# Eight output projections moved in among the last exponentials of the attention, with the divisor chain, the first routing slots and the key loads reordered around them

## The chip, the cores and the metric

One core of a Trainium2 chip (trn2). The metric is the device time of one execution in microseconds; lower is better. All four compute engines and the DMA queues run from their own instruction streams and meet only at semaphores.

## The reference, cut to what matters

Two transformer layers on x of shape (1, 2048, 256), all in float32. The change touches the end of the first layer's attention and the start of the second layer.

```python
xn = layernorm(x)                                    # over D = 256
q, k, v = split(xn @ w_qkv.T)                        # 16 heads of 16 columns
probs = softmax(mask(q @ k.T / 4))                   # causal, S = 2048
x = x + (probs @ v).reshape(S, 256) @ w_o.T + moe0(xn)   # top 2 of 16 experts
xn = layernorm(x)
probs = softmax(xn @ w_router); top 4 of 16 experts  # choices, weights
x = x + qn * sum(kn * v) + moe1(xn, choices) * 4/5 + (silu(xn @ ws1) * (xn @ ws3)) @ ws2 / 5
```

## The kernel before, in words

The kernel has three stages, each a block of five instruction streams. A block ends when every engine has reached its end.

**Stage one** (`stage_first`) computes the first layer. Tokens lie in 16 tiles of 128 and in four chunks c of 512; heads lie in four groups g of four. For each pair (g, c) it computes row maxima ("max" units: bf16 matmuls on TensorE, one `tensor_reduce` on VectorE), turns them ("turn"), and sends them by DMA into rows of the query tile (`rows_out`). Then come the exponentials: one "exp" unit is a score matmul for two heads and 128 keys (TensorE, into one of two banks `ps_st`), and one ScalarE `activation` of up to 1024 columns; one "pv" unit multiplies two such results by the values. There are 320 exps, numbered 1 to 320; (3, 3), the last pair, has 289 to 320. The units of the first expert layer (x, h, y, then fetch and sum) are threaded in between.

`attention_plan` works out one order of all units; every engine walks this same list and takes its own part of it in this order, so an instruction waits for all that stands ahead of it on its own engine. `with_shares` inserts further steps at given exp counts. These steps turn a chunk's raw head sums into attention output: for share n = (k, c), k = 0 or 1 being half of the heads, SyncE moves the softmax divisors out (`divisors_out`) and the heads to their place (`heads_home`), **gather** loads the divisors into `m.divisor` ([128, 32]), **invert** takes the reciprocal on VectorE, **return** stores it, **spread** loads it over the partitions in eight DMAs, and **share** multiplies on VectorE. There are eight shares (0 to 3: k = 0, 4 to 7: k = 1); the first seven are in stage one, and share 7 is in stage two.

SyncE walks the same list. A unit "exp" means nothing to it: it doesn't wait at one, so its DMAs leave as fast as the waits between them allow. At the turn of (g, 2), g at least 1, it waits for the values of group g - 1 and issues the six DMAs of `load_keys` for group g + 1 (each 256 KB, one for each of TERMS = 6 products of bf16 parts). For g = 1 there follow the two loads of the output weights `m.wo` (tensors `count` and `before`), and gather 0.

**Stage two** (`stage_second`) projects the 16 tiles of attention output (`project(i)`: two fp32 matmuls of 256 columns, and a VectorE addition to `m.x`), takes the second layer norm of each tile (VectorE `bn_stats`, `bn_aggr`; a square root on ScalarE in `root_of(c)`; `scales(c)` on VectorE; `normalize` on ScalarE), turns it (`turn`), scores it against the router (`score`, which waits for both DMAs of `w_in`: the router and `w_attn`), picks the experts (`best_of(c)`), counts ranks on TensorE (`ranks(c)`), and works out a slot in memory for every choice (`slots_of(c)`). GpSimd then sends every token row to its slots: 64 indirect DMAs, 16 for each chunk, which wait for `slots_ready` of that chunk and for nothing else but each other. TensorE meanwhile adds up a Gram matrix (`add_gram`) and does 16 units of the shared expert. When the 64 DMAs have landed, SyncE loads the first four tiles of rows (`m.xs`), and the block ends.

In stage two VectorE has this order, written by hand: tiles 0 to 4, scales 0, tiles 5 to 7, invert 7, tile 8, scales 1, tile 9, best_of 0, tile 10, share 7, slots_of 0, tile 11, tile 12, and so on. TensorE: project 0 to 6, turn 0 and 1, project 7, turn 2 and 3, project 8 and 9, score 0 to 3, project 10, add_gram 0 and 1, turn 4 and 5, ranks 0, add_gram 2, turn 6 and 7, project 11, score 4 to 7, project 12, and so on.

**Stage three** (`stage_experts`) runs the experts tile by tile and is not touched.

Of the kernel before, what the change touches and what calls it, by code (L numbers as in the profile page):

```python
# [333 lines left out]
def load_keys(eng, m, g, tokens, done):  # L334

    for t in range(TERMS):
        src = m.qk_parts[K_PART[t], D + g * HG * HD:D + (g + 1) * HG * HD, tokens]
        eng.dma_start(m.ks[g % 2][t * HD:(t + 1) * HD, :, tokens], src.rearrange("(h d) t -> d h t", d=HD)).then_inc(done, 16)
# [36 lines left out]
def common(nc, m):  # L375
# [30 lines left out]
    m.o_now, m.divisor = flat[:, 0:CH], m.r["slotf"][:, TOP0:TOP1, :].rearrange("p k i -> p (k i)")  # L406
# [267 lines left out]

SHARE_STEPS = (("gather", 3), ("invert", 13), ("return", 14), ("spread", 17), ("share", 28))
SHARES_FROM, SHARES_SPACE = 290, 2


def with_shares(plan):


    exps = [u for u in plan if u[0] == "exp"]
    due, at, n = [], 0, 0
    for u in plan:
        if u[0] == "exp":
            at += 1
        elif u[0] == "pv":
            g, c, k, _ = exps[2 * u[1]][1:]
            if g % 2 and k == TC * (c + 1) - 1 and n + 1 < len(SHARES):
                assert SHARES[n] == (g // 2, c)  # L690
                due += [(max(at + later, SHARES_FROM + SHARES_SPACE * n) if name == "share" else at + later, name, n)
                        for name, later in SHARE_STEPS]
                n += 1
    due.sort(key=lambda step: step[0])
    out, at = [], 0
    for u in plan:
        out.append(u)
# [8 lines left out]
NOT_ROWS = ("exp", "pv", "sum", "fetch", *(name for name, _ in SHARE_STEPS))  # L706
# [59 lines left out]
def stage_first(nc, m, a):  # L766
# [6 lines left out]
    row_of = {u[0:2]: n for n, u in enumerate(rows) if u[0] in "xhy"}  # L773
    rank_at = rows.index(("rank",))
    assert plan[TURNED - 1] == ("turn", 0, 0) and all(u[0] == "max" for u in plan[:TURNED - 1])
    with ExitStack() as ctx:
# [73 lines left out]
        def ends_pair(m):  # L850

            return exps[2 * m][3] == TC * (exps[2 * m][2] + 1) - 1
# [4 lines left out]

        def used(n):

            return sum(u[0] != "h" for u in rows[:n + 1])  # L860
# [8 lines left out]
        def _(sp):  # L869
# [19 lines left out]
            n = 0  # L889
            for u in plan:  # L890
                if u[0] == "pv" and ends_pair(u[1]):
# [8 lines left out]
                elif u[0] == "gather":  # L900
                    if u[1] == 0:
                        sp.wait_ge(slots_ready, TOP0 + 1)
                        for k in range(KH):
                            sp.dma_start(m.wo[k], a["w_o_t"][k * P:(k + 1) * P, :]).then_inc(m.wo_in, 16)
                    gather_divisors(sp, m, u[1])
                elif u[0] == "return":
                    return_divisors(sp, m, u[1])
                elif u[0] == "spread":
                    spread_divisors(sp, m, u[1])
                elif u[0] == "turn":  # L910
                    g, c = u[1:3]
                    if n:
                        rows_out(sp, n, c)
                    n += 1
                    if g + 1 < NG and c == (1 if g == 0 else 2):

                        if g >= 1:
                            sp.wait_ge(pv_done, last_pv(g - 1, C - 1))
                        load_keys(sp, m, g + 1, slice(0, S), k_in[(g + 1) % 2])
                    if (g, c) == (1, 0):  # L920

                        clear(sp, m, m.xd1, E * CAP // P, E * CAP // P + 1, m.cleared[1])
# [231 lines left out]
        def _(dve):  # L1154
# [73 lines left out]
            for u in plan:  # L1228
# [11 lines left out]
                if u[0] in ("pv", "gather", "return", "spread"):  # L1240
                    continue
                if u[0] == "sum":
# [16 lines left out]
                if u[0] == "x":  # L1259
# [40 lines left out]
        def _(pe):  # L1300
# [91 lines left out]
            for u in plan:  # L1392
# [44 lines left out]
                elif u[0] == "turn":  # L1437
# [3 lines left out]
                    mm = pe.transpose(bank[0:HG * TC, 0:P], neg_max[:, :], m.ident[:, :])  # L1441
                elif u[0] == "x":
# [287 lines left out]
def stage_second(nc, m, a):  # L1730
# [3 lines left out]
    with ExitStack() as ctx:  # L1734
# [68 lines left out]
        def _(sp):  # L1803
            last = len(SHARES) - 1
            divisors_out(sp, m, NG - 1, C - 1)
            sp.dma_start(wr[:, :, :], a["w_router"].rearrange("(k p) e -> p k e", p=P)).then_inc(w_in, 16)
# [51 lines left out]
        def _(act):  # L1858
# [14 lines left out]
            heads_home(act, m, NG - 1, C - 1)  # L1873
# [23 lines left out]
        def _(dve):  # L1897
# [23 lines left out]
            def project(i):  # L1921

                dve.wait_ge(w_done, i + 1)
                dve.tensor_tensor(m.x[:, i, :], ps_w[i % 2], m.x[:, i, :], ALU.add).then_inc(added, 1)
# [45 lines left out]
            slots_of(0)  # L1970
            tile(11)
            tile(12)
# [117 lines left out]
        def _(pe):  # L2090
# [31 lines left out]
            def project(tiles):  # L2122

                for i in tiles:
                    pe.wait_ge(m.shared, C + i // TC + 1)
                    if i >= 2:
                        pe.wait_ge(added, i - 1)
# [14 lines left out]
            project(range(10, 11))  # L2142
# [149 lines left out]
```

## Time and profile before

| | us |
|---|---|
| median of 3 runs | 903.83 |
| lowest, highest | 898.98, 904.56 |
| the profiled execution, its own time | 906.89 |
| its span in the trace | 905.2 |

| engine | busy us | share of the span |
|---|---|---|
| PE (TensorE matmul) | 830.5 | 92% |
| DVE (VectorE) | 645.3 | 71% |
| ACT (ScalarE) | 468.8 | 52% |
| POOL (GpSimd) | 437.1 | 48% |

Times in the trace count from the span's start. Stage one ends at 602, stage two at 731. The busy share is an average over stages that have different limits; what a change is worth is read where the change is. PEclk is the clock that TensorE was granted, 1.00 being 2.4 GHz and 0.50 being 1.2 GHz.

### The profile page before, as it was taken

What the parts mean: (1) busy time and instruction counts of PE and PEld (TensorE: products, weight loads), DVE (VectorE), ACT (ScalarE), POOL (GpSimd) and SP (SyncE); (2) the same over time, 40 slices, a digit from 0 to 9 for tenths busy, and PEclk for the clock granted to TensorE, in tenths of its full rate; (3) what the DMA queues carried; (4) which work ended last, traced back from release to release, by engine and by line L of the source; (5) the groups of instructions that cost most, each with busy time, mean ns of one, the idle gap of its engine ahead of it and who ended that gap; (6) DMA issues with size and microseconds to landing.
All of it is one profiled execution on the core that took longest, in us unless ns stands there. A gap on an engine that the chain in (4) does not pass through costs nothing. (4 is left out here: it accounts for less than half of the span.)

```text
span 905.2 us, 16683 instructions
## 1 busy us (share of the span) xinstructions
PE 830.5 (92%) x4934; PEld 449.4 (50%) x4935; DVE 645.3 (71%) x1472; ACT 468.8 (52%) x883; POOL 437.1 (48%) x720
## 2 busy tenths in 40 slices
PE   5978699999988999999999998989999989999993
PEld 3533133334533444444444432138644769888982
DVE  5587988898867888888788888437547336555648
ACT  2643154556654666666565666754313046555547
POOL 3422045603652433653435446531578848878820
PEclk9997698999998999999999999989999989999997
DMA  9654772210272121272211222325852235555566
GB/s 328 212 129 137 207 142 89 89 46 25 81 128 71 49 61 56 80 127 71 70 38 38 55 60 76 93 65 188 302 166 88 88 117 164 157 154 159 158 255 246
DMA packets 70182, 110.05 MB, mean 122 GB/s; under 512 B 16662, under 2 KB 49942, under 8 KB 69590
## 3 DMA queue, kind: packets, MB, share of 16 engines
q1 hardware_dynamic: 49430, 54.04, 22.9%
q0 software_dynamic: 16000, 45.70, 14.7%
q10 hardware_dynamic: 4672, 9.34, 3.4%
q8 instruction: 38, 0.62, 0.3%
q14 instruction: 42, 0.34, 0.1%
HBM read 62.53 MB, written 46.22 MB: 120 GB/s over the span
## 5 line engine op out<-in xcount | busy, mean ns | idle before, releaser
L1275 DVE TENSOR_REDUCE part_max<-ps_row 128x1 f32<-128x512 f32 (+3 forms) x560 | 353.6, 670 | 71.1 <-PE ps_row L1429 38.7
L1139 ACT ACTIVATE probs<-ps_st 128x1024 f32<-128x1024 f32 (+3 forms) x320 | 278.2, 896 | 204.6 <-PE ps_st L1408 188.2
L1333 PE MATMUL ps_o<-probs,v_all 128*17 128x512 f32 (+3 forms) x1280 | 150.4, 542 | 6.9 <-POOL probs L1009 5.6
L1429 PE MATMUL ps_row<-ks,qs 96*128 96x512 bf16 (+3 forms) x320 | 110.2, 379 | 13.7 <-DVE part_max L1275 9.3
L1429 PE MATMUL ps_row<-xt_ks,qs 96*128 96x512 bf16 (+3 forms) x320 | 104.5, 354 | 6.9 <-DVE part_max L1275 6.5
L1682 POOL DMA_INDIRECT yd<-moe_ys,moe_home x79 | 82.6, 1046 | 25.5 <-POOL moe_home L1676 13.4
L1408 PE MATMUL ps_st<-qs,ks 99*128 99x512 bf16 (+3 forms) x320 | 88.7, 360 | 2.9 <-DMA qs<-max_parts 2.7
L1408 PE MATMUL ps_st<-qs,xt_ks 99*128 99x512 bf16 (+3 forms) x320 | 85.7, 356 | 3.9 <-ACT probs L1139 2.8
L1702 PE MATMUL moe_ps_h<-moe_xs_t,moe_w_now 128*128 128x128 f32 x632 | 86.0, 280 | 1.3 <-ACT moe_xs_t L1607 0.8
L1702 PEld LDWEIGHTS moe_ps_h<-moe_xs_t,moe_w_now 128*128 128x128 f32 x632 | 78.4, 195 | 3.2 <-DVE moe_w_now L1569 2.0
L1429 PEld LDWEIGHTS ps_row<-ks,qs 96*128 96x128 bf16 x320 | 31.9, 100 | 95.6 <-DVE part_max L1275 52.8
L1009 POOL TENSOR_SCALAR_AFFINE_SELECT probs<-probs 128x256 f32<-128x256 f32 x128 | 52.8, 419 | 47.3 <-ACT probs L1139 46.0
L1851 POOL DMA_INDIRECT xd<-xn,slot x64 | 65.8, 1029 | 19.0 <-issue 15.9
L1019 POOL TENSOR_SCALAR moe_h_tanh<-moe_h_tanh 128x128 f32<-128x128 f32 x47 | 25.0, 532 | 98.7 <-ACT moe_h_copy L1151 98.5
L1429 PEld LDWEIGHTS ps_row<-xt_ks,qs 96*128 96x128 bf16 x320 | 31.0, 97 | 80.7 <-DVE part_max L1275 46.6
L1642 DVE TENSOR_TENSOR moe_hid_t<-moe_ps_h,moe_act 128x128 f32<-128x128 f32 x79 | 23.0, 291 | 47.7 <-ACT moe_act L1614 37.2
L997 POOL DMA_INDIRECT xd<-o_t,slot x32 | 31.4, 982 | 46.2 <-ACT probs L1139 41.7
L1432 PE MATMUL ps_row<-mask,ident 128*128 128x128 bf16 x256 | 51.7, 227 | 0.0
L1711 PE MATMUL moe_ps_y<-we,moe_hid_t 128*128 x158 | 48.6, 389 | 3.1 <-DVE moe_hid_t L1642 1.6
L1408 PEld LDWEIGHTS ps_st<-qs,xt_ks 99*128 99x128 bf16 x320 | 27.3, 99 | 47.8 <-ACT probs L1139 27.0
L1029 POOL DMA_DIRECT2D yd<-moe_ys x47 | 28.5, 605 | 46.1 <-DVE moe_ys L1267 45.4
L1333 PEld LDWEIGHTS ps_o<-probs,v_all 128*17 128x17 f32 x1280 | 21.7, 95 | 53.6 <-issue 29.0
(288 smaller groups left out, 1307.3 us busy)
## 6 DMA issues: line engine op xcount, KB each, us to landing
moe_xs<-xd SPq DMA_DIRECT2D x79, 129.0 KB
qk_parts<-probs SPq DMA_DIRECT2D x16, 384.0 KB, 4.2
qs<-qk_parts SPq DMA_DIRECT2D x96, 64.0 KB, 2.5
moe_xs<-xd POOLq DMA_DIRECT2D x47, 128.0 KB, 2.4
yd<-moe_ys POOLq DMA_DIRECT2D x47, 128.0 KB, 2.1
xd<-zeros POOLq DMA_DIRECT2D x2, 2048.0 KB, 15.5
moe_w<-in_w ACTq DMA_DIRECT2D x2, 2048.0 KB
w<-in_we SPq DMA_DIRECT2D x8, 512.0 KB
```

Of the source, the lines that this page charges most:

```text
L997: pool.indirect_dma_start(out=m.xd0, out_offset=bass.IndirectOffsetOnAxis(m.r["slot"][:, choice, i:i + 1], 0), in_=m.xn[:, i, :], in_offse ...
L1009: pool.affine_select(out=corner, in_=corner, compare_op=ALU.is_ge, fill=keep, base=0, pattern=[[0, 2], [1, P]], channel_multiplier=-1).the ...
L1139: act.activation(probs[:, at % NPB, :, off:CH], ps_st[at % 2][:, :, off:CH], ACT.Exp, scale=HD ** -0.5).then_inc(exp_done, 1)
L1275: dve.tensor_reduce(part_max[reduced % 2][:, h:h + k, i, j:j + 1], bank[:, 0:k * w].rearrange("p (h w) -> p h w", h=k), AX_X, ALU.max).the ...
L1333: mm = pe.matmul(ps_o[32 * q:32 * q + HD + 1, off:CH], m.v_all[:, k, g * HG + q, :], probs[:, (at + q // 2) % NPB, q % 2, off:CH], start=F ...
L1408: mm = pe.matmul(ps_st[n % 2][:, h, off:CH], ks[g % 2][:, q, k * P:(k + 1) * P], qs[c][:, q, off:CH], start=True, stop=True)
L1429: mm = pe.matmul(cols, qs[c][0:KROWS, h, i * P:(i + 1) * P], ks[g % 2][0:KROWS, h, j * CH:j * CH + w], start=True, stop=(j < c))
L1432: mm = pe.matmul(cols[:, w - P:w], m.ident16[:, :], m.mask16[:, :], start=False, stop=True)
L1682: pool.indirect_dma_start(out=yd, out_offset=bass.IndirectOffsetOnAxis(home[:, k:k + 1].bitcast(U32), 0), in_=ys[:, k % U, :], in_offset=N ...
L1702: mm = pe.matmul(ps_h[b][:, part * P:(part + 1) * P], w_now[:, b, k, part * HID:(part + 1) * HID], xs_t[:, b, k, :], start=(k == 0), stop= ...
L1711: pe.matmul(ps_y[b][:, :], hid_t[:, b, :], w2[:, bass.ds(expert, 1), :], start=True, stop=True).then_inc(y_done, 1)
L1851: pool.indirect_dma_start(out=m.xd1, in_=xn[:, i, :], in_offset=None, out_offset=bass.IndirectOffsetOnAxis(r["slot"][:, k, i:i + 1], 0)).t ...
```

## The change

Eight of the sixteen projections become plan units of stage one: `("project", i)` for tiles 0 to 7, after exps 297, 299, ... 311, in the row banks `ps_row`. Each adds to `m.x` on VectorE. Two units "moments" (after 306 and 313) do the `bn_stats` and `bn_aggr` of tiles 0 to 3 and 4 to 7 there. Shares 4, 1, 5, 2, 3, 6 get exp counts of their own. `m.divisor` gets memory of its own. In stage two the last heads move from ScalarE's queue to SyncE's, ahead of the router load, gather 7 and `w_attn`; TensorE starts with projections 8 and 9; VectorE starts with scales 0, and does slots_of 0 ahead of share 7. The six key DMAs of groups 2 and 3 are given exp counts three apart, and SyncE issues each when it meets that count in its list. By the list, the first two of group 2 come ahead of the output weights and gather 0, the next three behind gather 0, and the last behind return 0.

```diff
-SHARES_FROM, SHARES_SPACE = 290, 2
+KEY_SPACE = 3
+SHARES_AT = {0: 290, 4: 291, 1: 293, 5: 294, 2: 306, 3: 308, 6: 312}
+PROJECT_AT = (297, 299, 301, 303, 305, 307, 309, 311)
+MOMENTS_AT = (306, 313)
+BEFORE_LAST = len(PROJECT_AT)
...
-                due += [(max(at + later, SHARES_FROM + SHARES_SPACE * n) if name == "share" else at + later, name, n)
+                due += [(max(at + later, SHARES_AT[n]) if name == "share" else at + later, name, n)
...
+    due += [(at, "project", i) for i, at in enumerate(PROJECT_AT)] + [(at, "moments", c) for c, at in enumerate(MOMENTS_AT)]
...
             for u in plan:
-                if u[0] == "pv" and ends_pair(u[1]):
+                if u[0] == "exp":
+                    at += 1
+                    while pieces and pieces[0][0] <= at:
+                        _, g, t = pieces.pop(0)
+                        load_keys(sp, m, g, slice(0, S), k_in[g % 2], [t])
+                elif u[0] == "pv" and ends_pair(u[1]):
...
-                    if g + 1 < NG and c == (1 if g == 0 else 2):
-
-                        if g >= 1:
-                            sp.wait_ge(pv_done, last_pv(g - 1, C - 1))
-                        load_keys(sp, m, g + 1, slice(0, S), k_in[(g + 1) % 2])
+                    if (g, c) == (0, 1):
+                        load_keys(sp, m, 1, slice(0, S), k_in[1])
+                    if g + 1 < NG and g >= 1 and c == 2:
+
+                        sp.wait_ge(pv_done, last_pv(g - 1, C - 1))
+                        pieces += [(at + KEY_SPACE * t, g + 1, t) for t in range(TERMS)]
...
+                if u[0] == "moments":
+                    cs = slice(u[1] * TC, (u[1] + 1) * TC)
+                    dve.wait_ge(row_used, used(row_of["project", u[1] * TC + TC - 1]))
+                    for i in range(cs.start, cs.stop):
+                        step(dve.bn_stats(m.stat["bn"][:, i, :], m.x[:, i, :]))
+                    step.sync()
+                    for i in range(cs.start, cs.stop):
+                        step(dve.bn_aggr(m.stat["mv"][:, i, :], m.stat["bn"][:, i, :]))
...
+                if u[0] == "project":
+                    i = u[1]
+                    dve.wait_ge(summed, (i + 1) * TOP0)
+                    dve.tensor_tensor(m.x[:, i, :], bank[:, 0:D], m.x[:, i, :], ALU.add).then_inc(row_used, 1)
...
+                elif u[0] == "project":
+                    i = u[1]
+                    bank_free(n)
+                    pe.wait_ge(m.wo_in, 16 * KH)
+                    pe.wait_ge(m.shared, shares_upto(i // TC))
+                    for k in range(KH):
+                        mm = pe.matmul(bank[:, 0:D], m.o_t[:, 2 * k, i * P:(i + 1) * P], m.wo[k],
+                                       start=(k == 0), stop=(k == KH - 1))
...
             divisors_out(sp, m, NG - 1, C - 1)
+            heads_home(sp, m, NG - 1, C - 1)
             sp.dma_start(wr[:, :, :], a["w_router"].rearrange("(k p) e -> p k e", p=P)).then_inc(w_in, 16)
...
-            heads_home(act, m, NG - 1, C - 1)
...
-            for i in range(0, 5):
-                tile(i)
             scales(0)
-            for i in range(5, 8):
-                tile(i)
-            invert_divisors(dve, m, last)
             tile(8)
             scales(1)
             tile(9)
+            tile(10)
+            invert_divisors(dve, m, last)
             best_of(0)
-            tile(10)
-            share_heads(dve, m, last)
             slots_of(0)
             tile(11)
+            share_heads(dve, m, last)
             tile(12)
...
-            pe.wait_ge(m.wo_in, 16 * KH)
-            project(range(0, 7))
+            project(range(8, 10))
             turn(range(0, 2))
-            project(range(7, 8))
+            project(range(10, 11))
             turn(range(2, 4))
-            project(range(8, 10))
             pe.wait_ge(w_in, 32)
             pe.wait_ge(ones_ready, 1)
             score(range(0, 4))
-            project(range(10, 11))
             add_gram(range(0, 2))
```

## Rows read from the trace of the kernel before

**Rows 1.** Busy us of each engine (instructions), clock, DMA share, GB/s, by stretch.

```profile
268.20:274.20 6.00, 0.01 (x1) 0.01 (x1) 0.96 (x3) 0.39 (x1) 1.25 (x4) 0.86 0.69 154
274.20:280.20 6.00, 6.00 (x28) 2.96 (x29) 4.25 (x8) 1.93 (x3) 1.15 (x2) 0.57 0.23 67
```

**Rows 2.** Timeline of SyncE's queue: start, us, DMA issues and their count.

```profile
255.54 3.59 SPq L338 DMA_DIRECT2D ks<-qk_parts  x6
...
260.13 0.46 SPq L734 DMA_DIRECT2D slotf<-den  x1
```

**Rows 3.** DMA issues of 254 to 275: count, KB each, median us to landing.

```profile
ks<-qk_parts SPq DMA_DIRECT2D x6, 256.0 KB, 8.6
```

**Rows 4.** Timeline of the engines at 273 to 277; idle time before, and releaser, in brackets.

```profile
273.24 0.35 DVE L755 RECIPROCAL slotf<-slotf 128x32 f32<-128x32 f32 x1 [6.08 <-DMA slotf<-den]
...
274.19 0.61 PE L1429 MATMUL ps_row<-xt_ks,qs 96*128 96x512 bf16 x1 [6.00 <-DVE part_max L1275]
...
276.54 1.02 ACT L1139 ACTIVATE probs<-ps_st 128x1024 f32<-128x1024 f32 x1 [7.93 <-PE ps_st L1408]
```

**Rows 5.** Timeline of the last pair's exponentials, TensorE and ScalarE.

```profile
578.04 1.04 PE L1408 MATMUL ps_st<-qs,xt_ks 99*128 99x512 bf16 x4
...
578.69 3.89 ACT L1139 ACTIVATE probs<-ps_st 128x1024 f32<-128x1024 f32 x4 [0.26 <-PE ps_st L1408]
579.01 1.05 PE L1333 MATMUL ps_o<-probs,v_all 128*17 128x512 f32 x8
...
580.00 1.29 PE L1408 MATMUL ps_st<-qs,xt_ks 99*128 99x512 bf16 x4
...
587.18 3.77 ACT L1139 ACTIVATE probs<-ps_st 128x1024 f32<-128x1024 f32 x4 [2.40 <-remote]
```

**Rows 6.** Stretches, columns as in rows 1: exps 297 to 312, and stage two's second part.

```profile
574.53:594.87 20.34, 17.97 (x97) 3.18 (x96) 6.88 (x14) 15.40 (x17) 12.06 (x13) 0.92 0.32 92
...
647.90:727.20 79.30, 79.28 (x229) 42.42 (x225) 39.70 (x73) 16.16 (x24) 60.25 (x78) 1.00 0.35 118
```

**Rows 7.** Timeline of TensorE's projections, at the lower clock and at the full one.

```profile
605.03 1.06 PE L2129 MATMUL ps_ab<-before,o_t 128*128 128x256 f32 x2
...
608.21 0.59 PE L2129 MATMUL ps_o<-count,o_t 128*128 128x256 f32 x2
...
608.64 0.59 PE L2129 MATMUL ps_o<-before,o_t 128*128 128x256 f32 x2
```

**Rows 8.** Timeline of the DMA issues at the start of stage two.

```profile
602.81 2.57 ACTq L724 DMA_DIRECT2D o_t<-masks  x4
...
606.80 0.34 SPq L734 DMA_DIRECT2D slotf<-den  x1
...
607.18 0.43 SPq L1808 DMA_DIRECT2D w_attn<-in_w_attn  x1
```

**Rows 9.** DMA issues of 590 to 740: count, KB each, median us to landing.

```profile
w_attn<-in_w_attn SPq DMA_DIRECT2D x1, 768.0 KB, 4.6
```

**Rows 10.** Timeline from the square root's table to GpSimd's first dispatch.

```profile
605.42 1.28 ACT L1861 ACT_TABLE_LOAD   x1 [2.94 <-issue]
...
616.34 1.85 PE L2106 MATMUL ps_l<-w_router,xt 128*128 128x16 f32 x16
...
622.27 0.69 DVE L763 TENSOR_TENSOR o_t<-o_t 128x512 f32<-128x512 f32 x1 [1.46 <-DMA o_t<-rec]
...
624.80 0.17 DVE L280 CAST slot<-slotf 128x16 uint32<-128x16 f32 x1
...
625.12 0.19 POOL L1849 CAST xn<-home 128x2 f32<-128x2 int32 x1 [22.05 <-DVE slot L280]
```

**Rows 11.** Timeline of the end of stage two.

```profile
725.96 0.97 POOL L1851 DMA_INDIRECT xd<-xn,slot  x1 [0.30 <-issue]
...
728.66 1.95 SPq L1835 DMA_DIRECT2D moe_xs<-xd  x4
...
731.28 1.09 PE L1694 MATMUL moe_ps_x<-ident,moe_xs 128*128 128x128 f32 x4 [4.10 <-PEq L1734]
```

More of the change, by code:

```diff
@@ L331, with load_keys @@
 PB = 4
-def load_keys(eng, m, g, tokens, done):
-    for t in range(TERMS):
+def load_keys(eng, m, g, tokens, done, terms=range(TERMS)):
+    for t in terms:
         src = m.qk_parts[K_PART[t], D + g * HG * HD:D + (g + 1) * HG * HD, tokens]
@@ L405, in common @@
     flat = masks[:, TOP0:TOP1, :, :].rearrange("p k i e -> p (k i e)")
-    m.o_now, m.divisor = flat[:, 0:CH], m.r["slotf"][:, TOP0:TOP1, :].rearrange("p k i -> p (k i)")
+    m.o_now, divisor = flat[:, 0:CH], m.sb("divisor", [P, NH // 2 * CH // P])
+    m.divisor = divisor[:, :]
     m.wo = [m.r[name].rearrange("p e i -> p (e i)") for name in ("count", "before")]
@@ L705 @@
 SHARES = [(k, c) for k in range(2) for c in range(C)]
-NOT_ROWS = ("exp", "pv", "sum", "fetch", *(name for name, _ in SHARE_STEPS))
+NOT_ROWS = ("exp", "pv", "sum", "fetch", "moments", *(name for name, _ in SHARE_STEPS))
 def divisors_out(eng, m, g, c):
@@ L772, in stage_first @@
     turns = [u for u in plan if u[0] == "turn"]
-    row_of = {u[0:2]: n for n, u in enumerate(rows) if u[0] in "xhy"}
+    row_of = {u[0:2]: n for n, u in enumerate(rows) if u[0] in ("x", "h", "y", "project")}
     rank_at = rows.index(("rank",))
@@ L856, in masked_upto, with shares_upto @@
             return sum(u[3] >= TC * u[2] for u in exps[:at + 1])
+        def shares_upto(c):
+            order = [u[1] for u in plan if u[0] == "share"]
+            return 1 + max(order.index(SHARES.index((k, c))) for k in range(2))
         def used(n):
@@ L888, in _ @@
                          m.ones16[0:PARTS, :].unsqueeze(1).to_broadcast([PARTS, HG * T, P])).then_inc(ones_in[1], 16)
-            n = 0
+            n, at, pieces = 0, 0, []
             for u in plan:
-                if u[0] == "pv" and ends_pair(u[1]):
+                if u[0] == "exp":
[4 more added lines that the diff above has]
+                elif u[0] == "pv" and ends_pair(u[1]):
                     g, c = exps[2 * u[1]][1:3]
@@ L1241, in _ @@
                     continue
+                if u[0] == "moments":
[6 more added lines that the diff above has]
+                        step(dve.bn_aggr(m.stat["mv"][:, i, :], m.stat["bn"][:, i, :]))
+                    step.sync()
+                    step(dve.tensor_scalar(m.stat["var"][:, cs], m.stat["mv"][:, cs, 1], EPS, None, ALU.add))
+                    continue
                 if u[0] == "sum":
@@ L1258, in _ @@
                 bank = ps_row[n % NSM]
-                if u[0] == "x":
+                if u[0] == "project":
+                    i = u[1]
+                    dve.wait_ge(summed, (i + 1) * TOP0)
+                    dve.tensor_tensor(m.x[:, i, :], bank[:, 0:D], m.x[:, i, :], ALU.add).then_inc(row_used, 1)
+                elif u[0] == "x":
                     dve.tensor_copy(xs_t[:, u[1] % 2, :, :],
@@ L1921, in project @@
             def project(i):
-                dve.wait_ge(w_done, i + 1)
+                dve.wait_ge(w_done, i + 1 - BEFORE_LAST)
                 dve.tensor_tensor(m.x[:, i, :], ps_w[i % 2], m.x[:, i, :], ALU.add).then_inc(added, 1)
@@ L1957, in _ @@
             step(dve.tensor_scalar(given[:, 0, :, 0], m.iota_f[:, 0:E], float(CAP), None, ALU.mult))
-            for i in range(0, 5):
-                tile(i)
+            dve.sem_inc(added, BEFORE_LAST)
+            dve.sem_inc(bn_ready, BEFORE_LAST)
+            dve.sem_inc(mv_ready, BEFORE_LAST)
+            dve.sem_inc(std_wanted, BEFORE_LAST // TC)
             scales(0)
-            for i in range(5, 8):
-                tile(i)
-            invert_divisors(dve, m, last)
             tile(8)
@@ L2125, in project @@
                     pe.wait_ge(m.shared, C + i // TC + 1)
-                    if i >= 2:
+                    if i >= BEFORE_LAST + 2:
                         pe.wait_ge(added, i - 1)
```

## The prediction

> **What bounds the kernel now.** I read three places, each for the wait that ends last there, since the busy shares of the whole span say little. First the timeline around the key loads of group 2, because the change takes loads out of SyncE's queue ahead of gather 0. The engines stand still there: the reciprocal of invert 0 waits 6.08 us for its DMA, TensorE 6.00 us for VectorE behind it, ScalarE 7.93 us for TensorE [rows 4]. In the six microseconds to 274.20 TensorE was busy for 0.01, and in the next six it was fully busy but at 0.57 of its clock [rows 1]. The reader should see that this is one stall with one cause: SyncE issued six key DMAs at 255.54 and the gather only at 260.13 [rows 2], and the gather's data came 13.1 us later; the keys themselves took 8.6 us to land [rows 3].
>
> Second, the last exponentials. Four exps take 3.89 us on ScalarE with 0.26 idle, so a pair of exps takes 2.08 us. TensorE starts the pair's four score matmuls at 578.04, its value matmuls at 579.01 and the next scores at 580.00 [rows 5]: 1.96 us of a pair's 2.08. Both engines are nearly full. There is one hole: ScalarE stands for 2.40 us before 587.18, with a releaser that the trace can't name.
>
> Third, stage two. GpSimd starts its 64 dispatches at 625.12, after 22.05 us of waiting for the first slots, which end with the cast at 624.80 [rows 10]. Its last one begins at 725.96, SyncE loads the rows at 728.66 when they have landed, and stage three starts on TensorE at 731.28, after 4.10 us of standing [rows 11]. TensorE is full (79.28 of 79.30 us) up to 727.2 [rows 6], but it isn't what ends last: GpSimd's chain is, by a few microseconds. So stage two ends as much earlier as the first slots do, until TensorE becomes the bound.
>
> **The change part by part.** *Keys in pieces.* SyncE waits for no exp, so the spacing of three exps is no pacing; what counts is the order in the queue. Ahead of gather 0 now stand two keys (512 KB) and the output weights (256 KB) in place of six keys (1536 KB) and the weights. From the first key's issue to the reciprocal 17.7 us passed for 1792 KB [rows 2, 4]; with 768 KB ahead, in proportion, 7.6 us, so the divisors would be there near 263. VectorE comes to invert 0 at 273.24 - 6.08 = 267.2 [rows 4]. The wait goes, with some 4 us to spare, and what is late next is TensorE itself, which was full before the stall. Gain: 6.0 us of standing and 0.43 x 6.0 = 2.6 us of slow clock [rows 1], 8.6 together; from below, 5 if the gather still comes 2 or 3 us late, since a shorter stall may cost less clock too. The sixth key now stands behind return 0 and, for group 3, the last two stand behind spread 3. Who waits for them is the first row maximum of the next group, which lies some forty exps after the turn while the pieces lie within fifteen counts: nothing, unless SyncE is held there for more than ten microseconds.
>
> *Shares and divisor.* The same multiplications at other counts, and a buffer of its own: nothing.
>
> *Eight projections among the exps.* One is two matmuls that start 0.43 us apart [rows 7]: 0.86 us. One comes in each pair of exps, and makes TensorE's pair 1.96 + 0.86 = 2.82 us, over ScalarE's 2.08. So eight pairs take 22.6 us. They took 20.34 before [rows 6], of which 8 x 2.08 = 16.6 is the steady pace and 3.7 the hole and the low clock after it (0.92 in the stretch). If the projections fill the hole, the price is 22.6 - 20.3 = 2.3 us; if it comes on top in full, 6.0. Before ScalarE resumes TensorE can run just one projection ahead, so I take 4. VectorE gets eight additions and two sets of moments; at 6.88 us busy of 20.34 [rows 6] it has the room. Behind the moments in its queue stand the sums, behind these on GpSimd the fetches, and behind those the masks of the diagonal exps from 313 on; a sum is due only every three exps, so I cost this at nothing, and at 2 us if the moments hold the sums up longer than that.
>
> *The start of stage two.* The eight projections go from TensorE's head: there it was at the lower clock at first (1.06 us a pair of passes against 0.59 [rows 7]). Now projections 8 and 9 still take that slow opening. The square root's table load, 1.28 us [rows 10], which came behind ScalarE's four head issues (2.57 us [rows 8]), can begin at once, and the first four tiles are turned by about 610. But score 0 waits for `w_attn`. The four head issues now stand ahead of it on SyncE, whose own four divisor issues end near 604: the last head leaves near 606 instead of 604.8, so the gather goes near 608 instead of 606.80 and `w_attn` near 608.4 instead of 607.18 [rows 8]; it takes 4.6 us to land [rows 9]. Score 0 starts near 613 instead of 616.34 [rows 10]: 3.4 us earlier, after some 3 us of standing.
>
> *Slots ahead of share 7.* Before, slots 0 stood behind share 7, which itself waited for its DMA at 622.27 [rows 10]. Now they follow the scores, the ranks and their own 2 us. From the end of score 0: two tiles of Gram matrix and a turn on TensorE, 2.5 us, then ranks 0.4 and slots 2.1. With 1.85 us for score 0 that gives 619.9; if the clock is low after the standing, score 0 takes about twice as long: 621.5. GpSimd starts 3.4 to 5 us earlier; I take 4. Share 7 is then ready near 622, as before, and TensorE meets projection 12 a little earlier than before, by 2 to 3 us: with the few microseconds that it had in hand it doesn't pass GpSimd as the bound, or only just. Bounds for stage two: 2 to 5.5.
>
> **Sum.** -8.6 + 4 - 4 = -8.6 us against the profiled execution's own 906.89: 898.3. That execution lies 3.06 us above the median of 903.83, so I forecast 895.2 for the median, and write 895.5.
>
> **The rivals.** *The gather still comes late (A).* SyncE isn't held by exps, so keys three to five leave right behind the gather. If the DMA engines serve a queue's transfers side by side, five keys in flight hold the gather nearly as long as six, and the 8.6 us shrink to 2 or 3. For it: the transfers saturate the engines together. Against it: the keys, issued first, landed after a median of 8.6 us and the gather, issued last, after 13.1 [rows 3, 4]; that is the order of a line. Time: 895.5 + 6 = 901.5. The Trainium skill, "DMA: Bandwidth & Descriptors", section on queues, rings and completion order, says that each DMA engine consumes a queue's descriptors in ring order; by this the gather would pass the later keys, and I give A less for it.
>
> *Little comes of stage two and much is paid among the exps (B).* The hole comes on top in full (6 us) and the slow clock after the standing leaves 2 us of gain: 895.5 + 2 + 2 = 899.5. For it: ScalarE's hole has no cause that a projection would cure.
>
> *TensorE stays slow (C), the case on the other side.* The place is the opening of stage two. TensorE now has three projections there in place of eleven ahead of score 0, and stands twice. In rows 1 it stood for 6 us and then ran at 0.57 for the next six though fully busy. If after standing near 610 it ran at the lower clock all the way from 613 to 648, it would lose half of 35 us, 17.5, less a microsecond or so in hand: 895.5 + 16.5 = 912. The change turns into a loss once the low clock lasts 19 us or more. Against it: in the trace the low clock ends within six microseconds of full work. The Trainium skill, "TensorE: Matmul & The Clock Gate", in the section "What's actually happening", says that the throttled state is the default and activity releases it; by that rule dense work taken from the opening is what kept the clock, which is C's case, and rows 1 fit it as far as they go.
>
> *A key comes too late (D)*: the last pieces behind return and spread, a stall at the first maximum of a group. It needs over ten microseconds more on SyncE; within C's chance.
>
> **How the numbers follow.** The forecast has 0.55, A 0.17, B 0.18, C and D together 0.10. The forecast's own bounds: lowest 903.8 - 9 + 2.3 - 5.5 = 891.6, and with the hole absent in the runs a little under that; highest 903.8 - 5 + 6 - 2 = 902.8. To hold 8 in 10 I go from 888.5 to 904, which takes in A and B. One per cent, 9 us, is about what a measurement of this kernel can tell from no change; 894.8 lies close to my forecast. So: faster by over 1% 0.43 (a little under half of the forecast's cases and the low ones of the rest), within 1% 0.50, slower by over 1% 0.07.
>
> **What the changed kernel's profile would show.** Invert 0 with no wait on its DMA, and no stretch of idle TensorE near 268 to 274: the first step. Pairs of exps from 297 to 312 at 2.8 us with ScalarE waiting for scores in each: the second. Score 0 some 10 us after the start of stage two instead of 13.5, its wait ended by the `w_attn` DMA, and GpSimd's first dispatch 18 us after that start instead of 22: the third. In stage two's end GpSimd still last. The prediction is wrong if the reciprocal still waits (A), if the granted clock is 0.5 for long after score 0 (C), or if the projections cost more than TensorE's own time because VectorE is slow to free the banks.

## The result, and the profile after

| | before | after |
|---|---|---|
| median of 17 runs each, us | 903.83 | 902.42 |
| the profiled execution, its own time | 906.89 | 901.55 |
| its span in the trace | 905.2 | 899.8 |

The ratio of the runs is 0.9939, with a 95% interval from 0.991 to 0.9968. Six of the 17 runs of the kernel before, eight of the changed one's (all at 914 us or above) and later one of e_router_alone (1355.24 us) are slow ones; the ratios leave them out, the medians in the tables don't (without them the two above are 901.4 and 896.82 us). Run again beside other kernels (label e_after_again), the change had 0.994 [0.9916, 0.9964], 891.31 us against 897.47. So it gains 0.6%, some 5 us of 900. That is within one per cent, and two thirds of the 8.3 us that I forecast.

The stall of the reciprocal is gone, as predicted. SyncE's queue in the profile after (start, us, issues), to be read against [rows 2]:

```profile
256.73 1.72 SPq L338 DMA_DIRECT2D ks<-qk_parts  x2
258.50 0.42 SPq L920 DMA_DIRECT2D count<-in_w_o_t  x1
258.96 0.43 SPq L920 DMA_DIRECT2D before<-in_w_o_t  x1
259.44 0.43 SPq L740 DMA_DIRECT2D divisor<-den  x1
259.91 1.39 SPq L338 DMA_DIRECT2D ks<-qk_parts  x3
268.58 0.34 SPq L746 DMA_DIRECT2D rec<-divisor  x1
268.96 0.44 SPq L338 DMA_DIRECT2D ks<-qk_parts  x1
```

VectorE's timeline has the reciprocal with no wait ahead of it, and the stretches (columns as in [rows 1], whose two they replace) are full at the full clock:

```profile
268.21 0.34 DVE L761 RECIPROCAL divisor<-divisor 128x32 f32<-128x32 f32 x1
```

```profile
268.20:274.20 6.00, 5.95 (x49) 2.98 (x51) 5.84 (x13) 4.10 (x7) 3.49 (x8) 1.00 0.99 183
274.20:280.20 6.00, 6.00 (x38) 2.44 (x30) 4.91 (x9) 3.62 (x6) 1.33 (x3) 1.00 0.40 92
```

Among the last exponentials every pair now has its projection. ScalarE and TensorE in the timeline after, against [rows 5]:

```profile
568.12 1.02 ACT L1156 ACTIVATE probs<-ps_st 128x1024 f32<-128x1024 f32 x1
568.78 0.60 PE L1440 MATMUL ps_st<-qs,xt_ks 99*128 99x512 bf16 x2
...
569.31 1.05 PE L1365 MATMUL ps_o<-probs,v_all 128*17 128x512 f32 x8
569.41 1.02 ACT L1156 ACTIVATE probs<-ps_st 128x1024 f32<-128x1024 f32 x1 [0.28 <-PE ps_st L1440]
570.29 0.60 PE L1440 MATMUL ps_st<-qs,xt_ks 99*128 99x512 bf16 x2
...
570.74 0.60 PE L1480 MATMUL ps_row<-count,o_t 128*128 128x256 f32 x2
570.93 1.02 ACT L1156 ACTIVATE probs<-ps_st 128x1024 f32<-128x1024 f32 x1 [0.50 <-PE ps_st L1440]
571.17 0.59 PE L1480 MATMUL ps_row<-before,o_t 128*128 128x256 f32 x2
571.60 0.60 PE L1440 MATMUL ps_st<-qs,xt_ks 99*128 99x512 bf16 x2
```

ScalarE starts an exp at 568.12 and the same place of the next pair at 570.93: 2.81 us a pair, and it waits for scores before each of the two exps between, 0.28 and 0.50 us. The stretch that answers to the first of [rows 6] is 22.55 us long and TensorE is busy in all of it:

```profile
568.12:590.67 22.55, 22.55 (x129) 9.45 (x128) 12.70 (x34) 16.36 (x16) 12.51 (x13) 1.00 0.30 84
```

The opening of stage two on TensorE in the timeline after, against [rows 7, 10]:

```profile
598.76 0.67 PE L2169 MATMUL ps_o<-count,o_t 128*128 128x256 f32 x2 [1.01 <-PEq L782]
...
602.19 0.93 PE L2138 MATMUL ps_t<-ident,xn 128*128 128x128 f32 x4 [1.46 <-ACT xn L1911]
...
608.89 3.60 PE L2146 MATMUL ps_l<-w_router,xt 128*128 128x16 f32 x16 [4.11 <-DMA w_attn<-in_w_attn]
612.33 3.44 PE L2158 MATMUL ps_gram<-xn 128*128 128x257 f32 x8
...
621.26 0.70 PE L2169 MATMUL ps_o<-count,o_t 128*128 128x256 f32 x2 [0.56 <-issue]
621.80 0.74 PE L2169 MATMUL ps_o<-before,o_t 128*128 128x256 f32 x2
622.33 1.92 PE L2158 MATMUL ps_gram<-xn 128*128 128x257 f32 x4
624.04 1.06 PE L2169 MATMUL ps_ab<-count,o_t 128*128 128x256 f32 x2
```

Score 0 waits 4.11 us for `w_attn` and then takes 3.60 us where it took 1.85 [rows 10]. Near 622 TensorE falls to the lower level once more: 1.06 us for a pair of passes that takes 0.59 [rows 7]. The first slots and the end of the stage, from VectorE, GpSimd and SyncE, against [rows 10, 11]:

```profile
618.40 0.17 DVE L280 CAST slot<-slotf 128x16 uint32<-128x16 f32 x1
618.71 0.19 POOL L1890 CAST xn<-home 128x2 f32<-128x2 int32 x1 [19.73 <-DVE slot L280]
...
720.48 0.97 POOL L1892 DMA_INDIRECT xd<-xn,slot  x1 [0.31 <-issue]
723.18 1.95 SPq L1876 DMA_DIRECT2D moe_xs<-xd  x4
724.59 0.69 DVE L2032 TENSOR_TENSOR o_t<-ps_ab,gate 128x512 f32<-128x512 f32 x1 [2.55 <-PE ps_ab L2220]
725.83 0.63 PE L1734 MATMUL moe_ps_x<-ident,moe_xs 128*128 128x128 f32 x4 [1.35 <-PEq L1774]
```

To compare kernels I use three marks, all read in the timeline: ScalarE's copy of the raw heads of pair (3, 2), that of (3, 3), and TensorE's first matmul of stage three. Before, they lie at 566.05, 601.88 and 731.28; after, at 558.93, 597.81 and 725.83. So the first part is 7.12 us shorter, the last exponentials 3.05 longer (38.88 in place of 35.83), stage two 1.38 shorter (128.02 in place of 129.40), and what follows equal (173.9 and 174.0). The sum is the 5.4 us between the spans. The experiments take these parts to pieces.

### The profile page after: what moved, and what is told of

Read it like the earlier page. It is cut to its first block and busy times, and to the rows that moved or that the text cites. A ratio compares the mean times of both kernels' runs of the same rounds, so it can differ in the third digit from the quotient of the medians.

```text
span 899.8 us, 16690 instructions
## 1 busy us (share of the span) xinstructions
PE 829.7 (92%) x4934; PEld 451.0 (50%) x4935; DVE 643.0 (71%) x1472; ACT 469.5 (52%) x883; POOL 438.5 (49%) x720
```

## The experiments

Ratios are to the kernel before, run on the same chip in the same session; there its median was 896.86 us for the first four, 897.47 for the next four and 896.32 for the last three. "Exps" is the time from the copy of (3, 2) to that of (3, 3), "stage two" that from there to stage three.

| kernel | us | ratio, 95% interval | exps | stage two |
|---|---|---|---|---|
| e_keys_only | 886.25 | 0.9891 [0.9868, 0.9914] | 30.48 | 129.33 |
| e_gather_first | 886.26 | 0.9882 [0.9863, 0.9901] | 30.48 | 129.52 |
| e_keys_together | 901.28 | 1.0056 [1.0031, 1.0081] | 37.83 | 126.92 |
| e_router_alone | 887.82 | 0.9915 [0.9884, 0.9945] | 36.54 | 123.13 |
| e_after_again | 891.31 | 0.994 [0.9916, 0.9964] | 36.63 | 127.28 |
| e_filler | 888.34 | 0.9894 [0.9865, 0.9923] | 36.50 | 124.47 |
| e_four | 884.99 | 0.9861 [0.9837, 0.9885] | 35.54 | 122.60 |
| e_double | 897.95 | one run | 45.89 | 126.14 |
| e_none | 888.83 | 0.9892 [0.9849, 0.9936] | 32.86 | 127.59 |
| e_four_again | 884.6 | 0.9881 [0.984, 0.9921] | 33.10 | 124.36 |
| e_heads_scalar | 889.61 | 0.9936 [0.9911, 0.9962] | 36.53 | 126.34 |

**Only the keys (e_keys_only).** The kernel before with SyncE's part of the change alone:

```diff
+                if u[0] == "exp":
+                    at += 1
+                    while pieces and pieces[0][0] <= at:
+                        _, g, t = pieces.pop(0)
+                        load_keys(sp, m, g, slice(0, S), k_in[g % 2], [t])
```

> The kernel before with the key pieces alone (SyncE's order around gather 0 and the later turns). Theory of the queue's order: the 6 us wait of invert 0 and the low clock after it are all that the keys cost, so it is 7 to 8.5 us faster than the kernel before, the reciprocal starts right behind the row maxima, and stage two stays as it was. Rival A (five keys in flight hold the gather almost as long as six): 2 to 3 us faster, with a wait of 3 us or more left ahead of the reciprocal. Rival 'given back': the keys that land later stall a row maximum of the next group, and less than 4 us come out.

**The gather first (e_gather_first).** The kernel before with the six keys of group 2 in one piece, but behind the output weights and gather 0:

```diff
                     gather_divisors(sp, m, u[1])
+                    if u[1] == 0:
+                        load_keys(sp, m, 2, slice(0, S), k_in[0])
...
-                        load_keys(sp, m, g + 1, slice(0, S), k_in[(g + 1) % 2])
+                        if g != 1:
+                            load_keys(sp, m, g + 1, slice(0, S), k_in[(g + 1) % 2])
```

> The kernel before with the output weights and gather 0 ahead of all six keys of group 2, which then leave together; nothing is in pieces. Theory of the queue's order: what counts is only what stands ahead of the gather, so this is as fast as the pieces, 7 to 8.5 us faster than the kernel before. Rival of the pieces (it is the spreading of the keys that relieves the engines): little or nothing, under 3 us, since all six keys are in flight at once.

**The keys together (e_keys_together).** The changed kernel with the keys as they were:

```diff
-                        pieces += [(at + KEY_SPACE * t, g + 1, t) for t in range(TERMS)]
+                        load_keys(sp, m, g + 1, slice(0, S), k_in[(g + 1) % 2])
```

> The changed kernel with the six keys issued together as before; all else of the change stays. If the keys are the whole gain and the rest gives back some of it, this is 0 to 4 us slower than the kernel before (projections among the exps cost 2 to 6 us, stage two returns 1 to 2). If my sum was right on the rest (cost 4, gain 4), it is within 1 us of the kernel before. The wait of 6 us ahead of the first reciprocal is back in both cases.

The first two gain 1.1 and 1.2% and the third loses 0.6%: by the ratios the keys' order gives 9.8 and 10.6 us of 896.86 on the kernel before (I had put 7 to 8.5), and the third lies 1.2 points, some 10 us, above the changed kernel. Without its keys the change is thus a loss of 5 us, where I had put 0 to 4. With everything it has a ratio of 0.994, and the keys alone have 0.9891; the two intervals (up to 0.9914, from 0.9916) are of different sessions and just don't overlap, so the rest of the change looks like a loss here as well. Spreading has no part in it, since six keys in one piece behind the gather gain as much. The DMA views of 254 to 272 show why. The gather of the divisors in e_keys_only, e_gather_first and e_keys_together (count, KB, median us from issue to landing):

```profile
slotf<-den SPq DMA_DIRECT2D x1, 16.0 KB, 5.5
```

```profile
slotf<-den SPq DMA_DIRECT2D x1, 16.0 KB, 1.8
```

```profile
divisor<-den SPq DMA_DIRECT2D x1, 16.0 KB, 13.3
```

Three or six keys right behind it don't hold it up (it has 768 KB ahead in the first case and 256 KB in the second); with 1792 KB ahead, six keys and the output weights, it takes 13.3 us, and the stall is back on VectorE in e_keys_together:

```profile
274.58 0.35 DVE L761 RECIPROCAL divisor<-divisor 128x32 f32<-128x32 f32 x1 [6.40 <-DMA divisor<-den]
```

Rival A falls. The Trainium skill, "DMA: Bandwidth & Descriptors", section on queues, rings and completion order, has each DMA engine consume a queue's descriptors in ring order; the 1.8, 5.5 and 13.3 us agree with it.

**The router on its own (e_router_alone).** The changed kernel, but `w_attn` counts on a semaphore of its own, and score 0 waits for the router alone; what uses `w_attn` waits for it later.

```diff
-            sp.dma_start(w[:, :, :], a["w_attn"].rearrange("(k p) o -> p k o", p=P)).then_inc(w_in, 16)
+            sp.dma_start(w[:, :, :], a["w_attn"].rearrange("(k p) o -> p k o", p=P)).then_inc(wa_in, 16)
...
-            pe.wait_ge(w_in, 32)
+            pe.wait_ge(w_in, 16)
```

> The changed kernel with a semaphore of its own for w_attn, so that the first scores wait for the router alone. Theory: the 4.1 us of standing ahead of score 0, and the lower clock that follows it (score 0 in 3.6 us, the first Gram matmuls in 3.4), are what stage two lacks against my forecast; score 0 then starts 6 to 7 us after the stage's start instead of 10.2, the slots come 5 to 6 us earlier than in the changed kernel, and the whole is 4 to 6 us faster than the changed kernel, 9 to 11 us faster than the kernel before. Rival (share 7 is the bound): TensorE meets projection 12 earlier, waits there for share 7 instead, the clock falls there, and under 2 us come out.

Stage two falls to 123.13 us, 4.2 under e_after_again. TensorE doesn't stand ahead of score 0, and that runs at the full clock in its timeline; a second wait appears behind it, for share 7:

```profile
598.78 1.86 PE L2147 MATMUL ps_l<-w_router,xt 128*128 128x16 f32 x16
...
610.54 0.70 PE L2170 MATMUL ps_o<-count,o_t 128*128 128x256 f32 x2 [2.09 <-DVE o_t L769]
...
612.83 1.06 PE L2170 MATMUL ps_ab<-count,o_t 128*128 128x256 f32 x2
```

The 4 us are the trace's. The times give less than I had put: the ratio of 0.9915 is 7.6 us under the kernel before, not 9 to 11, and a quarter of a per cent under the changed kernel, with overlapping intervals. Part of what the wait cost has moved to share 7, as the rival had it.

**The changed kernel again, and with filler (e_after_again, e_filler).**

> The changed kernel as it is, once more, beside the other three. Every theory gives what was measured before: a ratio to the kernel before of 0.991 to 0.997, and the same marks in the profile (copy of head group (3,2) to that of (3,3) some 38 us, from there to stage three some 128 us, score 0 about 11 us after the start of stage two and 3.6 us long). It is the measure for the other three, and tells whether the marks repeat from one execution to the next.

```diff
+            for k in range(9):
+                pe.matmul(ps_g[0][:, 0:D], m.ident[:, :], xn[:, 0, 0:D], start=True, stop=True)
             pe.wait_ge(w_in, 32)
```

> The changed kernel with nine further float32 matmuls of 256 columns each in TensorE's queue just ahead of its wait for the router's and the attention weights. They compute nothing that is used, into a bank that the first Gram matrix overwrites. They fill the standing of 4.1 us ahead of score 0 without moving the w_attn load. Theory 'the low clock after the standing is what costs': score 0 takes 1.9 us in place of 3.6 and the two Gram matrices about 1.9 in place of 3.4, granted clock about 1.0 up to 618, GpSimd's first dispatch 3 us earlier and the kernel 2.5 to 3.5 us faster than the changed kernel. Rival 'only the wait for w_attn costs': the kernel's time stays within 1 us, because GpSimd's first dispatch hangs on VectorE and ScalarE rather than on the matmuls. Third possibility: the clock goes low nevertheless, and nothing moves.

TensorE in the timelines of e_after_again and, behind it, e_filler:

```profile
605.45 3.60 PE L2146 MATMUL ps_l<-w_router,xt 128*128 128x16 f32 x16 [3.74 <-DMA w_attn<-in_w_attn]
608.89 3.77 PE L2158 MATMUL ps_gram<-xn 128*128 128x257 f32 x8
```

```profile
601.09 4.05 PE L2178 MATMUL ps_gram<-xn,ident 128*128 128x256 f32 x18
604.98 1.88 PE L2146 MATMUL ps_l<-w_router,xt 128*128 128x16 f32 x16
606.71 1.98 PE L2158 MATMUL ps_gram<-xn 128*128 128x257 f32 x8
```

The same wait for `w_attn` is covered by work that computes nothing, and the two steps behind it take 3.9 us in place of 7.4, counted by their durations. Stage two is 2.8 us shorter (124.47 against 127.28), and the time 3.0 us (888.34 against 891.31, same chip; the intervals of the ratios just overlap). The theory of the slow clock is borne out; the rival, that only the wait costs, is not. The 2.8 us are a net figure: from score 0 to the next scores TensorE takes 6.79 us with filler and 10.95 without, 4.2 less, but with filler its clock falls later, at 614.19 behind a wait of 0.56 us for share 7, where in e_after_again it doesn't, and that takes 1.7 back. The Trainium skill, "TensorE: Matmul & The Clock Gate", section "What's actually happening", has the throttled state as the default and activity as what releases it; the filler agrees.

**Doubled projections (e_double).**

```diff
-                    for k in range(KH):
+                    for k in 2 * list(range(KH)):
                         mm = pe.matmul(bank[:, 0:D], m.o_t[:, 2 * k, i * P:(i + 1) * P], m.wo[k],
```

> The changed kernel with the matmuls of the eight projections among the exps issued twice (four in place of two, the same sum twice over, so those eight tiles take a doubled projection; the rest of the computation works on the changed values). Theory 'TensorE's own time sets the pair of exps from 297 to 312': each pair takes 2.82 + 0.86 = 3.68 us, and the stretch from the copy of (3,2) to that of (3,3) is 6.9 us longer than in the changed kernel. Rival 'the price is VectorE's, which frees the banks late, or ScalarE's': the pairs stay at about 2.8 us and the stretch grows by under 2 us.

What that text says of the output is wrong: the second pass starts the sum afresh, so the output is that of the changed kernel. ScalarE in its timeline:

```profile
569.39 1.02 ACT L1156 ACTIVATE probs<-ps_st 128x1024 f32<-128x1024 f32 x1 [1.14 <-PE ps_st L1440]
570.91 1.02 ACT L1156 ACTIVATE probs<-ps_st 128x1024 f32<-128x1024 f32 x1 [0.50 <-PE ps_st L1440]
573.07 1.02 ACT L1156 ACTIVATE probs<-ps_st 128x1024 f32<-128x1024 f32 x1 [1.14 <-PE ps_st L1440]
```

A pair takes 573.07 - 569.39 = 3.68 us, as expected to the hundredth. The exps grow by 9.3 us; 6.9 is what eight times 0.86 gives, and the other 2.4 is a hole of the size that sets e_four's two executions apart (last section). TensorE's own time sets the pair.

**Four, and none, among the exps (e_four, e_none, e_four_again).** Both have the router's own semaphore. e_four has projections at counts 297, 301, 305 and 309 and the other twelve in stage two, e_none has all sixteen there; in both invert 7, slots 0 and share 7 were set anew among VectorE's tiles (slots 0 behind tile 9, share 7 behind tile 11), and so was the order of TensorE's projections in stage two.

```diff
-PROJECT_AT = (297, 299, 301, 303, 305, 307, 309, 311)
+PROJECT_AT = (297, 301, 305, 309)
```

> The changed kernel with two edits: the attention weights count on a semaphore of their own, so that score 0 waits for the router's weights alone, and only four of the projections stand among the last exponentials (counts 297, 301, 305, 309), the other twelve in stage two. Theory 'a projection among the exps costs 0.75 us there, because TensorE's pair becomes 2.82 us against ScalarE's 2.07': the stretch from the copy of (3,2) to that of (3,3) is 33.5 us (36.5 with eight, 30.5 with none); stage two, to stage three's start, 122 to 124 us, since the four projections find room behind the first slots. The time: 3 us under that of the run with eight and the own semaphore, ratio to before about 0.988. Rival 'TensorE's total work decides in both places': a projection taken out of the exps costs in stage two what it saves there, stage two 126 us, ratio as with eight, 0.9915.

> As the run with four projections among the last exponentials and a semaphore of their own for the attention weights, but with none there: all sixteen projections in stage two, slots 0 still ahead of share 7. Theory 'two places, two prices': among the exps each projection costs 0.75 us, in stage two the first ones lie ahead of score 0 and delay GpSimd's first dispatch by 0.43 to 0.86 each less what ScalarE and VectorE need anyway. So the stretch from the copy of (3,2) to that of (3,3) falls from 33.4 (without the hole of 2.15) to 30.5, and stage two grows from 122.6 to 124 to 126: together 0.5 us faster to 1 us slower than with four. Rival 'every projection costs the same wherever it stands because TensorE is the bound of stage two too': stage two 126 us, no difference to four. Second rival 'stage two has slack to spare': stage two stays at 122.6 to 123.1 and the kernel is 2.5 to 3 us faster than with four, ratio to before 0.983.

> The kernel with four projections and the own semaphore once more, on the same chip as the one with none. Both theories: a ratio of 0.984 to 0.988 to the kernel before, stage two 122.6 us; the stretch of the last exps 33.4 us, or 35.5 where TensorE's clock falls at the turn to the last piece, as it did in its first profile.

Among the exps the price is steady: 30.5 us with none (32.86 less a hole of 2.4), 33.1 with four, 36.5 with eight, which is 0.65 to 0.75 each. In stage two none has 127.59 and four 122.60 and 124.36, where I had put 124 to 126 for none. With none, score 0 starts 13.2 us after the copy (604.44 less 591.23), with four 7.7, and TensorE is at the lower clock around 601 to 604, behind a wait of 2.1 us for ScalarE. The 5.0 us between none and e_four are about the four projections' own time, 3.5 (four times 0.87), and the 1.7 that the low clock costs there. So where the clock doesn't fall, a projection costs 0.87 in stage two and 0.65 to 0.75 among the exps: the rival that it costs the same in both places is not far off, and the rest hangs on a fall of the clock that can come and go from one execution to the next (last section). Exps and stage two together take 157.5 and 158.1 us with four, 159.7 with eight (e_router_alone) and 160.5 with none, 158.1 less its hole. That four are a better share than none or eight is therefore not shown. In one session the medians are 884.6 with four and 888.83 with none, with overlapping intervals of their ratios. e_four had the lowest ratio of the study, 0.9861. Against e_keys_only (0.9891, other session) it isn't told apart by the intervals.

**The last heads back on ScalarE (e_heads_scalar).**

```diff
             divisors_out(sp, m, NG - 1, C - 1)
-            heads_home(sp, m, NG - 1, C - 1)
...
+            heads_home(act, m, NG - 1, C - 1)
             for c in range(C):
```

> The changed kernel with the moving of the last heads given back to ScalarE. Theory 'the four head issues on SyncE hold w_attn back by 1.2 us and free ScalarE of 2.6 us': w_attn is issued 1.2 us earlier, but the table load and the first normalised tiles come 2.6 us later, so that the first four tiles are turned only about when the weights land; score 0 starts 0 to 1 us earlier than in the changed kernel, TensorE stands less ahead of it, and stage two is 127 to 128 us: no difference that shows. Rival 'the move to SyncE was worth its 2.6 us': score 0 starts 1.5 us or more later and stage two is 129 to 130.

Its ratio, 0.9936, is that of the changed kernel. The wait only changes its name, in TensorE's timeline:

```profile
600.02 1.18 PE L2138 MATMUL ps_t<-ident,xn 128*128 128x128 f32 x4 [4.08 <-ACT xn L1910]
...
603.55 3.43 PE L2146 MATMUL ps_l<-w_router,xt 128*128 128x16 f32 x16
```

TensorE stands 4.08 us for the normalised tiles ahead of turn 0 in place of 4.11 for `w_attn` ahead of score 0, and is at the lower clock behind it either way. Stage two is 126.34 us, a little under the 127 to 128 that I had put. That part of the change is worth nothing that the interval, some 2 us to either side, can tell.

## Why the prediction was right, and where its sizes were off

The median of 902.42 us is 6.9 above the forecast of 895.5, and 903.83 times the ratio, 898.3, is 2.8 above it; both lie inside the range. The mechanism held for the keys and among the exps, and in stage two it failed in two steps; the gain was two thirds of the forecast. That it came so near is in part luck: the keys gave over a microsecond more than their term, while each of the other two terms came out some 2 us worse. By its steps:

*The keys, 8.6 us.* Right, and a little small. The stall is gone for the stated reason, the order in the queue. From span start to the copy of (3, 2) it is 8.87 us in e_keys_only (557.18 for 566.05), and 9.8 by the ratio. One trace doesn't fix it to a microsecond: that copy lies between 555.43 and 558.93 in the eleven executions without the stall, which is 7.1 to 10.6 us ahead of the one before. That SyncE's counts are no pacing was right too. The shares, the divisor's own buffer and slots 0 ahead of share 7 weren't tried by themselves.

*The projections among the exps, 4 us.* The pair at 2.82 us was right, the term was not. I set it against the 20.34 us of [rows 6], with ScalarE's hole in it, and let the projections fill a part of the hole. But the hole seems to belong to that one execution: e_keys_only and e_gather_first, without a projection there and with the same code from there on, take 30.48 us where the profiled execution before took 35.83. There is no second trace of the kernel before to settle it. Against the steady pace the projections cost 6.0 us (36.5 for 30.5), the upper bound, as rival B had it. In the profile after 38.88 - 36.5 = 2.4 us of the exps are such a hole again, at another place.

*Stage two, -4 us.* It gave 1.38 in the profile, 2.1 in e_after_again. Two steps failed. First, the clock. I gave projections 8 and 9 the slow opening, but they ran at the full clock (0.59 to 0.67 us for what takes 0.59). And I let it be low for score 0 at most. It was low through most of the Gram matrices behind it as well (3.44 and 3.77 us for 1.98), and the filler shows what that costs: 4.2 us by score 0 and what follows it, 2.8 net. The wait itself I had foreseen (3 us; 4.11 came), and that score 0 moves forward (3.4 us; 14.46 - 11.08 = 3.4 came, counted from the copy). GpSimd's first dispatch came 20.90 us after the copy in place of 23.24: 2.3 us earlier and not 4. Second, what ends last, and with it that stage two ends as much earlier as the first slots do. I wrote that TensorE wouldn't pass GpSimd, or only just. To the start of the shared expert's 16 units, whose length is the same in both, TensorE's window from the copy is, before and after:

```profile
601.88:647.87 45.99, 42.94 (x257) 36.53 (x257) 31.23 (x159) 16.34 (x39) 13.11 (x20) 0.96 0.67 232
```

```profile
597.81:645.16 47.35, 39.31 (x224) 33.53 (x225) 24.23 (x133) 16.22 (x39) 15.28 (x23) 0.89 0.69 235
```

Eight projections of 0.86 us, 6.9 us, left this window, yet TensorE's busy time fell by just 3.6, since the rest ran slower (clock 0.89 for 0.96), and it stood 8.04 us in place of 3.05. So TensorE came 1.36 us later, and lost the 2.74 us that it had in hand before: from the window's end to stage three are 80.67 us after and 83.41 before, and 80.66 or 80.67 again in e_four, e_none and e_router_alone. The sum, 2.74 - 1.36 = 1.38, is what stage two gave. GpSimd's own chain would have given no more: SyncE's load of the rows behind it came 125.37 us after the copy in place of 126.78, 1.4 earlier and not 2.3, because its dispatches, from the first cast to the last start, took 101.8 us in place of 100.8; why isn't known. The two chains end nearly together in the profile after (SyncE's load is issued by 725.13, VectorE's last gate done by 725.28). In e_after_again GpSimd's is still the later, 721.30 against 721.15, from the timeline:

```profile
719.35 1.95 SPq L1876 DMA_DIRECT2D moe_xs<-xd  x4
720.46 0.69 DVE L2032 TENSOR_TENSOR o_t<-ps_ab,gate 128x512 f32<-128x512 f32 x1 [2.74 <-PE ps_ab L2220]
```

So GpSimd's chain alone no longer sets the end. The moved work was paid for among the exps, and in TensorE's window more was lost again than had left it: 3.3 us to the lower clock and 5.0 to standing, for 6.9.

*The rivals.* A fell. B's first half (the full 6 us) came true and so, nearly, did its second (2 us of gain from stage two; 1.4 to 2.1): 899.5 was the better sum. C's mechanism was there, but for about 7 us behind score 0 and some 3 near 622 and not 35, and the full clock came back during dense work. (Ahead of score 0 stood ten projections before, not eleven as C has it.) D: no stall at the next group's first maximum is seen; the copy of (3, 2) has the full gain of the keys.

With the terms as measured, -8.9 + 6.0 - 1.4 is -4.3 us, and -9.8 + 6.0 - 2.1 is -5.9; the runs say 0.6% of 900, 5.5.

## What to carry to other kernels

A hole in one profiled execution is no room: before work is costed as filling it, look whether it has a cause in the code, or take the steady pace on either side as the base. Work taken from an engine's opening is won only if what then stands ahead of that engine is ready as well; here one semaphore shared by a small load that was needed and a large one that wasn't kept TensorE standing for 4 us, and the low clock behind it cost some 3 to 4 more. In this DMA queue it was the order that counted, not the spreading: put the 16 KB that an engine waits for ahead of the megabyte that nobody needs yet.

## What the runs showed of the hardware that I had not expected

Two executions of the same kernel differ by where TensorE's clock falls. e_four and e_four_again are one kernel. At the turn from (3, 2) to (3, 3), after 2.14 and 2.24 us of work in four, the one was granted the lower level of 1.2 GHz, the other stayed at 2.4 GHz; stretches of e_four, then of e_four_again, columns as in [rows 1]:

```profile
554.00:558.00 4.00, 2.14 (x20) 0.66 (x20) 2.73 (x4) 1.94 (x2) 3.26 (x5) 0.87 0.32 93
558.00:562.00 4.00, 4.00 (x17) 0.73 (x13) 2.26 (x4) 2.52 (x3) 2.09 (x3) 0.50 0.28 81
```

```profile
554.00:558.00 4.00, 2.24 (x20) 0.78 (x16) 2.97 (x5) 2.60 (x4) 3.41 (x5) 1.00 0.22 67
558.00:562.00 4.00, 3.97 (x25) 0.70 (x23) 2.65 (x6) 3.73 (x4) 1.99 (x3) 1.00 0.33 92
```

ScalarE waits 2.15 us for scores behind it, and the exps take 35.54 us in place of 33.10. The other execution had its fall in stage two instead, near 610, behind a wait of 0.60 us for share 7, and lost 1.8 us there. So a hole of two or three microseconds comes and goes with no change in the code. Why the clock falls in one and not in the other isn't settled.

One more thing stays open. SyncE's load of the sorted rows, which ends GpSimd's chain, stood 1.4 or 1.5 us behind VectorE's last gate (before, e_keys_only, e_gather_first), 1.1 to 1.4 ahead of it (the changed kernel twice, e_keys_together, e_filler, e_four, e_double, e_heads_scalar), or 4.2 ahead (e_router_alone, e_none, e_four_again), and never between. I know of no semaphore that ties the two chains in that part, and what puts their ends into steps of some 2.8 us was not tried.
